# Storing the attention output of four heads as one tile of 128 partitions, in a two-phase attention and mixture-of-experts kernel

## What is computed

```
q, k, val = heads(xn @ Wq + bq), heads(xn @ Wk + bk), heads(xn @ Wv + bv)     # 16 heads of 16
pos       = sinusoid @ Wp + bp
score     = ((q + u) . k + relative_shift((q + v) . pos)) / 4
attention = softmax(score) @ val @ Wo + bo
experts   : each of 8 experts takes the 256 most probable of 1024 tokens,
            gelu(xin @ w1) @ w2 times the probability, added at their places
```

## Time and profile before

| | us |
|---|---|
| median of 3 executions | 4703.37 (4697.26 to 4705.75) |
| the profiled execution | 4700.11 |
| its span, first to last instruction | 4698.3 |

### The profile page before, as it was taken

How to read it: one execution, slowest core, us unless ns; L and a number is a source line. 1 busy time by engine, 2 the same in 40 slices (tenths; PEclk the granted TensorE clock), 3 DMA queues, 4 the chain that set the end, 5 groups by cost and what they waited for, 6 DMA issues and landing times. The chain is left out here.

```text
span 4698.3 us, 122852 instructions
## 1 busy us (share of the span) xinstructions
PE 4345.4 (92%) x48308; PEld 3356.0 (71%) x48308; DVE 3677.5 (78%) x7571; ACT 3393.9 (72%) x5153; POOL 1241.4 (26%) x905
## 2 busy tenths in 40 slices
PE   7899999999999999998999898889999999999997
PEld 3466666666666666666666666668888888888886
DVE  7699999989999899999998998855665666644455
ACT  3599999989999898999999999844444444444454
POOL 0111111111111111111111111125556656544443
PEclk9899999999999999999999999989999999999999
DMA  8899999999999999999999999972555555433259
GB/s 313 339 391 389 387 388 392 387 385 391 390 386 385 381 394 384 389 392 391 386 395 385 385 392 390 384 249 53 131 138 124 138 124 137 107 56 87 47 169 316
DMA packets 467846, 1391.25 MB, mean 296 GB/s; under 512 B 59216, under 2 KB 136656, under 8 KB 467024
## 3 DMA queue, kind: packets, MB, share of 16 engines
q1 hardware_dynamic: 418128, 1316.25, 74.2%
q0 software_dynamic: 49152, 67.14, 8.4%
HBM read 708.93 MB, written 674.23 MB: 294 GB/s over the span
## 5 line engine op out<-in xcount | busy, mean ns | idle before, releaser
L761 DVE CUSTOM_DVE_ANT_0 att_shifted<-att_quad,att_shifted 128x512 f32<-128x512 f32 x2048 | 1337.6, 684 | 112.4 <-DMA att_shifted<-xs_d 75.7
L614 ACT ACTIVATE att_shifted<-att_shifted,att_mn 128x512 f32<-128x512 f32 x2048 | 1375.7, 732 | 0.9 <-DVE att_mn L761 0.9
L609 ACT ACTIVATE ring<-att_quad 128x1024 f32<-128x1024 f32 x1024 | 1055.1, 1030 | 257.8 <-PE att_quad L988 244.1
L999 PE MATMUL att_quad<-att_kd,att_qd 64*128 64x512 f32 x2048 | 848.0, 459 | 179.6 <-DVE att_mn L761 173.8
L1434 ACT ACTIVATE ffn_hp<-ffn_up 128x512 fp32r<-128x512 f32 x512 | 305.9, 597 | 845.4 <-PE ffn_up L1615 845.1
L1520 DVE TENSOR_TENSOR ffn_hp<-ring,ffn_hp 128x512 fp32r<-128x512 f32 x512 | 460.3, 899 | 570.2 <-ACT ring L1436 570.0
L988 PE MATMUL att_quad<-att_pos,att_qd 64*128 64x512 f32 x2048 | 861.7, 448 | 15.0 <-ACT ring L609 13.6
L1024 PEld LDWEIGHTS att_tp<-ident,att_shifted 64*128 64x128 f32 x8192 | 645.6, 142 | 272.2 <-ACT att_shifted L614 117.7
L1615 PE MATMUL ffn_up<-ffn_xp,ffn_w1p 128*128 128x512 f32 x3072 | 796.3, 395 | 2.8 <-DVE ffn_xp L1463 2.8
L1024 PE MATMUL att_tp<-ident,att_shifted 64*128 64x64 f32 x8192 | 725.5, 229 | 64.4 <-DVE att_pt L770 23.0
L1025 PE MATMUL att_tp<-ident,att_shifted 64*128 64x64 f32 x8192 | 774.9, 232 | 2.3 <-issue 2.1
(11 more groups left out here) (132 smaller groups left out, 5931.9 us busy)
## 6 DMA issues: line engine op xcount, KB each, us to landing
xs_d<-ring SPq DMA_DIRECT2D x1024, 513.0 KB, 8.5
att_shifted<-xs_d SPq DMA_DIRECT2D x1024, 512.0 KB, 8.8
att_shifted<-in_L_attn_x_dram SPq DMA_DIRECT2D x32, 512.0 KB, 7.4
xn_d<-att_shifted SPq DMA_DIRECT2D x32, 512.0 KB, 6.7
xt_d<-att_shifted SPq DMA_DIRECT2D x32, 512.0 KB, 8.0
gathered<-xt_d SPq DMA_DIRECT2D x32, 512.0 KB, 9.7
att_d<-att_osb SPq DMA_DIRECT2D x512, 32.0 KB
ring<-in_L_ffn_w_dram SPq DMA_DIRECT2D x16, 1024.0 KB, 6.9
```

Source lines behind the costliest of these rows:

```text
L609: act.activation(xo[:, kk % NW, 2 * half:2 * half + 2, 1:S + 1], xp[:, :, :], ACT.Copy).then_inc(x_out, 1)
L614: act.activation(shifted[:, kk % NX, t], shifted[:, kk % NX, t], ACT.Exp, bias=mn[:, kk % NX, t:t + 1], scale=-1.0).then_inc(exp_done, 1)
L761: dve.tensor_tensor_reduce(out=shifted[:, kk % NX, t], in0=sp_[:, t % 2], in1=shifted[:, kk % NX, t], scale=-0.25, scalar=-NEG, op0=ALU.ad ...
L999: pe.matmul(sp_[:, t % 2, :], qd[rows, n // GH % ND, t * P:(t + 1) * P], kd[rows, kk // GH % 2, :], start=True, stop=True).then_inc(s_full, 1)
```

## The change

`att_d` becomes a list of tiles, one of [128, 512] per quad (128 quads), and `sums_d` goes. SP stores the whole of `osb`'s half in one transfer of 128 partitions x 2048 B; the rows that belong to nobody are stored with it. The feed-forward phase then picks what it needs out of the tiles: the sums as rows 16, 48, 80 and 112 of each tile (so the sums' tile in SBUF is ordered quad, t, head, token), the inverse stored to the unchanged `inv_d` in four transfers, one for each t, and a batch of attention in sixteen transfers, one for each head, of 16 partitions x 4 rows of 512 B. The semaphores' values follow. Left out of the diff are the signatures and calls, which lose `sums_d`.

```diff
@@ -423,15 +423,9 @@
 
                 def store_o(i, q):
 
-                    wait_alone(sp, o_out, i * QUADS + q + 1)
-                    at = bass.ds(i * 2 + q // NQ, 1)
-                    dst = att_d[at].rearrange("o (q h v) t -> (o q) v h t", q=NQ, h=QH)
-                    for t in range(TT):
-                        sp.dma_start(dst[q % NQ, :, :, t * P:(t + 1) * P], osb[32 * t:32 * t + HD, q % 2]).then_inc(o_stored[q % 2], 16)
-                    for t in range(TT):
-                        row = 32 * t + HD
-                        sp.dma_start(sums_d[at].rearrange("o (q h) t -> (o q) h t", q=NQ)[q % NQ:q % NQ + 1, :, t * P:(t + 1) * P],
-                                     osb[row:row + 1, q % 2]).then_inc(o_stored[q % 2], 16)
+                    u = i * QUADS + q
+                    wait_alone(sp, o_out, u + 1)
+                    sp.dma_start(att_d[u], osb[:, q % 2].rearrange("p h n -> p (h n)")).then_inc(o_stored[q % 2], 16)
 
                 sp.wait_ge(p_low, DC)
                 sp.wait_ge(w_low, 1)
@@ -471,7 +465,7 @@
                 store_o(ITERS - 1, QUADS - 2)
                 store_o(ITERS - 1, QUADS - 1)
                 for k in range(2):
-                    sp.wait_ge(o_stored[k], B * NQ // 2 * 2 * TT * 16)
+                    sp.wait_ge(o_stored[k], B * NQ // 2 * 16)
 
             @block.gpsimd
             def _(pool):
@@ -626,7 +620,7 @@
                     u = i * QUADS + q
                     act.wait_ge(o_full, (u + 1) * QH)
 
-                    wait(act, o_stored[q % 2], (u - q % 2) * (TT * 16))
+                    wait(act, o_stored[q % 2], (u - q % 2) // 2 * 16)
                     act.activation(osb[:, q % 2].rearrange("p h t -> p (h t)"), op[:, :], ACT.Copy).then_inc(o_out, 1)
 
                 act.wait_ge(edge_set, 1)
@@ -1264,23 +1258,28 @@
                     wait_alone(sp, w2_low, e * 2)
                     load_second(sp, w2, e, w2s).then_inc(w2_in, 16)
 
-                flat = "b (g h) t -> (b g) (h t)"
-                sp.dma_start(sums[:, :], sums_d.rearrange(flat, g=P // B)).then_inc(sums_in, 16)
+                sum_rows = att_d.rearrange("u (t r) n -> u t r n", t=TT)[:, :, HD]
+                sp.dma_start(sums.rearrange("p (t n) -> p t n", t=TT), sum_rows).then_inc(sums_in, 16)
                 sp.wait_ge(cleared, 1)
                 for g in range(NG):
                     rows = ffn_d[g * GB * S:(g + 1) * GB * S].rearrange("(p k r) d -> p k (r d)", p=P, r=TT)
                     sp.dma_start(rows, zero.unsqueeze(1).to_broadcast([P, GB * S // P // TT, TT * D])).then_inc(zeroed[g], 16)
                 sp.wait_ge(inverted, 1)
-                sp.dma_start(inv_d.rearrange(flat, g=P // B), sums[:, :]).then_inc(inv_stored, 16)
+                for t in range(TT):
+                    of_t = inv_d.rearrange("b (q h) s -> (b q) h s", h=QH)[:, :, t * P:(t + 1) * P]
+                    sp.dma_start(of_t, sums[:, t * QH * P:(t + 1) * QH * P].rearrange("p (h n) -> p h n", h=QH)).then_inc(inv_stored, 16)
                 sp.dma_start(wo[:, :, :], Wo.rearrange("(c p) n -> p c n", p=P)).then_inc(wo_in, 16)
                 sp.dma_start(bob[:, :], bo.partition_broadcast(P)).then_inc(wo_in, 16)
                 load_w(1)
-                sp.wait_ge(inv_stored, 16)
+                sp.wait_ge(inv_stored, TT * 16)
 
                 def load_mid(b, s):
 
                     wait_alone(sp, a_low, b - 1)
-                    sp.dma_start(att[:, s], att_d[bass.ds(b, 1)].rearrange("o (c p) t -> p (o c) t", p=P)).then_inc(m_in[s], 16)
+                    for h in range(H):
+                        rows = att_d[b * NQ + h // QH].rearrange("(t r) n -> r t n", t=TT)[0:HD, :, h % QH * P:(h % QH + 1) * P]
+                        at = h % (H // DC) * HD
+                        sp.dma_start(att[at:at + HD, s, h // (H // DC)].rearrange("p (t n) -> p t n", t=TT), rows).then_inc(m_in[s], 16)
                     for c in range(DC):
                         of_c = inv_d[bass.ds(b, 1), c * (H // DC):(c + 1) * (H // DC)]
                         sp.dma_start(inv[:, s, c], of_c.rearrange("o h t -> (o h) t").unsqueeze(1).to_broadcast([H // DC, HD, S])
@@ -1367,7 +1366,7 @@
 
                 def prepare(b):
 
-                    pool.wait_ge(m_in[b % 2], (b // 2 + 1) * 64)
+                    pool.wait_ge(m_in[b % 2], (b // 2 + 1) * (H + DC + 1) * 16)
                     pool.tensor_tensor(att[:, b % 2], att[:, b % 2], inv[:, b % 2], ALU.mult).then_inc(divided, 1)
                     pool.tensor_tensor(xi[:, b % 2], xi[:, b % 2], bob[:, :].unsqueeze(1).to_broadcast([P, TT, D]), ALU.add).then_inc(biased, 1)
 
@@ -1636,8 +1635,7 @@
     xt_d = nc.dram_tensor("xt_d", [B, P, DC, S], F32).ap()
     ffn_d = nc.dram_tensor("ffn_d", [B * S, D], F32).ap()
     xs_d = nc.dram_tensor("xs_d", [S * P + 8 * S * (S + 1)], F32).ap()[S * P:].rearrange("(k n) -> k n", k=8)
-    att_d = nc.dram_tensor("att_d", [B, D, S], F32).ap()
-    sums_d = nc.dram_tensor("sums_d", [B, H, S], F32).ap()
+    att_d = nc.dram_tensor("att_d", [B * NQ, P, QH * P], F32).ap()
     inv_d = nc.dram_tensor("inv_d", [B, H, S], F32).ap()
     mid_d = nc.dram_tensor("mid_d", [B, S, D], F32).ap()
     weights = {"Wq": Wq, "Wk": Wk, "Wv": Wv, "Wp": Wp, "bq": bq, "bk": bk, "bv": bv, "bp": bp,
```

More of the change, by code:

```diff
@@ L137, in shape_constants, with attention_phase @@
     return sinusoid, ident, marks, spread
-def attention_phase(nc, x, gate_w, w, w1, w2, consts, xn_d, xt_d, xs_d, att_d, sums_d, shared):
+def attention_phase(nc, x, gate_w, w, w1, w2, consts, xn_d, xt_d, xs_d, att_d, shared):
     sin_d, ident_d, marks_d, spread_d = consts
@@ L1162, with ffn_phase @@
 CONST_LOADS = 1 + DC + 2 + 4 + 5 + 1
-def ffn_phase(nc, x, Wo, bo, w1, w2, xn_d, shared, ffn_d, att_d, sums_d, inv_d, mid_d, out):
+def ffn_phase(nc, x, Wo, bo, w1, w2, xn_d, shared, ffn_d, att_d, inv_d, mid_d, out):
     MIX = 1
@@ L1647, in build @@
         attention_phase(nc, x, gate_w, weights, w1, w2, (c["sinusoid"], c["ident"], c["marks"], c["spread"]), xn_d, xt_d, xs_d,
-                        att_d, sums_d, shared)
-        ffn_phase(nc, x, Wo, bo, w1, w2, xn_d, shared, ffn_d, att_d, sums_d, inv_d, mid_d, out)
+                        att_d, shared)
+        ffn_phase(nc, x, Wo, bo, w1, w2, xn_d, shared, ffn_d, att_d, inv_d, mid_d, out)
 _INS = ["L0_attn_x", "L0_attn_Wq", "L0_attn_bq", "L0_attn_Wk", "L0_attn_bk", "L0_attn_Wv", "L0_attn_bv", "L0_attn_Wp",
```

## The result

The kernel after takes 4719.24 us (median of six executions, 4716.12 to 4729.3) beside 4700.74 us for the kernel before: ratio 1.0042, 95% interval 1.0032 to 1.0053. It is slower, by 18.5 us, where 59.5 us less was forecast. Its profiled execution has a span of 4715.9 us against 4698.3.

A forecast was written before the change was run, and what follows sets the result against it. DMA at a 410 GB/s ceiling was taken to bound the attention half, TensorE the feed-forward half. Attention -58, its end -2.5 and mixing groups +1 gave -59.5 us, about 4644 us against a 4703.37 median; range 4605 to 4690.

The forecast's parts named there:

- the stores' bytes count in full: Rival, attention half: the dip stays behind any store and 123 thousand more bytes a quad cost +38 us, about 4741; chance 0.08.
- What the store costs now: Attention half, old store: dip of 1.04 us plus 0.34 us for its bytes, 1.38 us of DMA engines per quad.
- limit (a): Attention half, DMA engines at 410 GB/s: 21.61 us per quad, 0.85 us less, 109 us over 128 quads.
- Limit (b): Attention half, VectorE: if its waits for loads vanished and others stayed, 0.57 us less per quad, 73 us over 128.
- End of attention: Last output copy to next phase: with one issue only the landing and handover remain, -2.5 us, between 0 and -3.
- SyncE's issue: Attention stores: one issue replaces eight, SyncE's part falling from 5.0 us to about 0.5 us.
- Mixing groups: Feed-forward half: sixteen loads a batch add 8 us on SyncE; GpSimd waits 6 us, TensorE covered, +1 us in all.
- The rule on small transfers: Skill page's rule: coalesce, under 64 KB mostly overhead is paid; taken to favour the store and oppose the sixteen 32 KB loads.

The follow-up runs named there:

- half: Kernel after, storing only two of the four heads' columns (131 thousand bytes a quad, one issue): 4679.36 us, 0.9961 of the kernel before.
- a quarter: Kernel after, storing only one head's columns of four (66 thousand bytes a quad, one issue): 4662.9 us, 0.9909 of the kernel before.
- e2_twice: Kernel after, with every output tile stored a second time to a scratch tensor (262 thousand bytes more a quad): 4801.68 us, 1.0225 of the kernel before.

## Why the prediction was wrong

The forecast was -59.5 us and the sign is wrong; what came is the rival "the stores' bytes count in full", to which I gave 0.08. It priced 123 thousand bytes at +38 us. Measured are +26.3 in the attention half and +18.5 in all. The 11 us between 38 and 26 are what eight issues and 272 packets had cost.

- **The step that failed is "What the store costs now": 1.38 us of the DMA engines per quad for 139 thousand bytes.** I read a flat 410 GB/s as a ceiling, took everything below it behind the burst as the store's cost, and priced a packet at 5 ns. The real cost is the bytes. From half to full to double the attention grows by 40.1 us and 79.8 us for 131 and 262 thousand bytes a quad: 0.316 and 0.628 us, 415 and 417 GB/s. At 415 GB/s the bytes of the old store cost 0.34 us and those of the new one 0.63. With 0.09 us for eight issues and 272 packets (next point) the old store cost 0.43 us, not 1.38. So the change costs 0.20 us a quad, where limit (a) had put a gain of 0.85.
- **The shortfall against 410 doesn't belong to the store.** Take 8737 thousand bytes with the old store, as in the prediction, exchange the store, and divide by 415: a quad is 20.88 + 1.24 us (a quarter), 21.03 + 1.21 (half), 21.35 + 1.21 (after), 21.98 + 1.21 (twice), 21.05 + 1.30 (before). For half, after and twice the second term is the same because 415 was fitted to them; the quarter and the kernel before test it. It stays within 0.03 us, and is 0.09 us more with eight issues and 272 packets. Limit (a) counted on 0.85 us of it and the forecast on 0.45 (58/128); 0.09 were won. The size of the term is not well known. With the 86 us of e2_twice's median the rate from after to twice is 386 GB/s, and from half to twice 398, at which the term would be 0.3 us; the 0.1 us more in the kernel before stays. (The 8737 goes with the 22.46 us counted in whole quads; with the 22.36 us of the copies it is 8698, and every second term is 0.09 larger.)
- **Limit (b), VectorE's waits for the loads, was read as if the burst caused them.** One stood 15 us behind it, but they don't go with the burst: 67.0 us before, 77.2 for a quarter, 68.7 for half, 90.4 after, 135.7 for twice. Together with the waits for TensorE's spreading they follow the bytes: 134 us for a quarter, 142 half, 145 before, 175 after, 247 twice. The two lines of e2_twice:

```profile
DVE att_shifted L758 <- DMA att_shifted<-xs_d: 135.7, 137, 3.6
DVE att_qd L731 <- PE att_mp L915: 111.7, 162, 1.8
```

- **End of attention:** -2.5 forecast, -2.8 measured. Right: from the end of the last copy to the next phase it took 2.96 us, where 3.0 for the landing and about 0.3 for the handover had been put.
- **SyncE's issue:** one issue in place of eight came as forecast, at a median of 0.763 us instead of 0.5. It was worth next to nothing, for SyncE only waits longer.
- **Mixing groups:** +1 forecast, +1.2 measured. That the two agree is luck: 1.2 us is within the scatter of the half, and the cause that I gave, 2 us of lateness behind the weights, did not come. The rest was right: GpSimd waits 5.9 us each time (175.8/30) where I said about 6, and TensorE is busy 843.20 of 844 us in these groups (3278 to 4122 us). Behind the first weights GpSimd multiplies at 3333.84 and ScalarE splits at 3341.53 without a wait:

```profile
3333.84 2.40 POOL L1370 TENSOR_TENSOR ffn_heads<-ffn_heads 128x1024 f32<-128x1024 f32 x1 [9.01 <-DMA ffn_tokens<-in_L_attn_x_dram]
...
3341.53 1.06 ACT L1416 ACTIVATE ffn_attp<-ffn_heads 128x1024 fp32r<-128x1024 f32 x1
```

  The issue of the loads ran while the weights were still landing: x, the last of them, is now issued 6.4 us before the product (3327.42) and was 13.5 us before it (3303.17). So 8 us more on SyncE made the wait only 1 us longer (7.99 in the earlier trace rows).
- **The rule on small transfers** ("DMA: Bandwidth & Descriptors" of the Trainium skill, section "Rules for kernel authors", to coalesce them) holds here in its direction only. Against one store of the same bytes (half's 2825.5 us plus 2.5 for 8 thousand bytes) eight stores cost 5 us of 2840 in 68 packets and 11 us in 272. The rule says nothing of sending unused rows along, and at 415 GB/s 123 thousand unused bytes a quad cost 38 us.

What stays open is the shortfall itself, and why it moves with the issues. SyncE waits for ScalarE's copies (L411) in every version. But that the low places are moments with nothing to move is not shown, and the share speaks against it as the whole cause: it is 1.00 at 373 GB/s, 0.99 at 351 and 0.92 at 328. No run took that apart.

Open is also how the bytes become time. TensorE's mean granted clock in the steady stretch falls with them, from 0.97 of full speed (half) to 0.96 (after) and 0.94 (twice), and its busy time per quad rises from 20.27 to 20.44 and 20.65 us (busy time of the stretch by its number of quads). So up to half of the first step and a third of the second could be TensorE's slower work rather than the wait for bytes; no run separates the two.

## What to carry to other kernels

When the DMA share stands at 1 through a stage and its mean rate doesn't move, price a change there by its bytes at the marginal rate (bytes added over time added), and get that rate by storing something twice. A dip in the rate just behind the traffic under suspicion isn't its price: here a shortfall that the stage has anyway only changed its place when the issues changed. Padding a transfer to a full tile pays only where the DMA engines have time; here storing just the 68 useful rows in five transfers takes 0.17% less than the kernel before and 0.6% less than the kernel after.

## What the runs showed of the hardware

- 384 more packets a quad, 512 rows of 512 B against 128 of 2 KB, cost at most 8 us in 2866; the price of 5 ns a packet would have made it 240.
- The mean rate hardly changes (388 to 390 GB/s) between stores of 66 and of 524 thousand bytes a quad. The marginal rate is 415 to 417 GB/s by the profiled executions and 386 to 398 by the medians, so that it lies above the mean is not shown.
- Sixteen loads of 32 KB take SyncE 8.13 us together, 0.5 us each, where one of 512 KB took 0.43. They overlap and are not sixteen latencies in a row: from the first issue to the product, with the loads behind them, it is 17.2 us:

```profile
3574.08 8.13 SPq L1282 DMA_DIRECT2D ffn_heads<-att_d  x16
3582.25 1.22 SPq L1285 DMA_DIRECT2D ffn_heads<-inv_d  x2
3583.52 0.45 SPq L1288 DMA_DIRECT2D ffn_tokens<-in_L_attn_x_dram  x1
...
3591.29 2.40 POOL L1370 TENSOR_TENSOR ffn_heads<-ffn_heads 128x1024 f32<-128x1024 f32 x1 [3.54 <-DMA ffn_tokens<-in_L_attn_x_dram]
```
